# A graph layer and slice attention on one core: 35 gathers a pair of windows, halved vector operations, filler matmuls in the tail, and a wait ahead of every nine gathers

## The reference, cut to what matters

```python
# block 1
n = layernorm(x)
agg = segment_sum(n[src], dst, 6250)              # 106250 edges
h = relu(agg @ W_rel + b_rel + n @ W_root)        # 256 -> 512
i, f, g, o = split(h @ W_ih.T + b_ih + b_hh, 4)   # 512 -> 2048; f is not used
c = sigmoid(i) * tanh(g)
x = x + (sigmoid(o) * tanh(c)) @ W_fc + b_fc
# block 2, 8 heads of 64, 64 slices each
n = layernorm(x)
w = softmax((n @ W_x + b_x) @ W_slice / temp)     # slice weights per node and head
token = (w.T @ (n @ W_fx + b_fx)) / (w.sum(nodes) + 1e-5)
out_slice = attention(token W_q, token W_k, token W_v)   # 64 x 64 per head
x = x + (w @ out_slice) @ W_out + b_out
```

## Time and profile before

| | |
|---|---|
| median of 3 runs | 1493.12 us (1491.98 to 1493.93) |
| the profiled execution | 1490.67 us, its span 1488.7 us |
| TensorE matmuls busy | 1225.3 us, 82% |
| GpSimd busy | 975.0 us, 65% |
| VectorE busy | 820.7 us, 55% |
| ScalarE busy | 584.7 us, 39% |
| mean granted clock of TensorE | 0.94 of full speed |
| first and last gather start | 87.07 and 1291.05 us |

### The profile page before, as it was taken

The page is one execution under the profiler, slowest core; times in us unless marked ns, Lnnn a source line. Parts: engine busy times, 40 slices in busy tenths (PEclk is TensorE's granted clock), DMA queues, the critical chain, the costliest instruction groups (busy, mean ns, idle before and its releaser), DMA issues.

```text
span 1488.7 us, 25194 instructions
## 1 busy us (share of the span) xinstructions
PE 1225.3 (82%) x8343; PEld 1075.8 (72%) x8343; DVE 820.7 (55%) x2125; ACT 584.7 (39%) x1120; POOL 975.0 (65%) x975
## 2 busy tenths in 40 slices
PE   0226898889988898889888998989888988894796
PEld 0214787878877787778777887878777877783596
DVE  3852364656455655566555655565556645554464
ACT  3631344434443444344443444344434434352131
POOL 1247777777777777777777777777777777500043
PEclk9997999999999999999999999999999999996698
DMA  5764444444444344444444444434444444203396
GB/s 150 230 202 131 113 122 130 124 125 119 134 118 132 111 135 125 127 122 121 135 118 126 118 134 120 133 110 134 125 125 120 124 134 131 88 29 98 96 344 206
DMA packets 109102, 198.03 MB, mean 133 GB/s; under 512 B 39587, under 2 KB 66079, under 8 KB 109052
## 3 DMA queue, kind: packets, MB, share of 16 engines
q0 software_dynamic: 46160, 124.60, 29.1%
q1 hardware_dynamic: 59312, 60.26, 13.8%
q10 hardware_dynamic: 3600, 12.80, 2.1%
HBM read 165.56 MB, written 32.87 MB: 133 GB/s over the span
## 4 chain that ended last, share of the span: by engine, by line
POOL 41%; issue 30%; DMA 13%; PE 10%; DVE 3%; SPq 1%; ACT 1%; POOLq 0%; DVEq 0%; ACTq 0%
POOL ring L545 41%; DMA ring<-table,sidx 10%; PE ps L296 3%; PE ps L298 2%; PE ps L297 2%; DMA table<-ring 1%; DMA ring<-dstp 0%; SPq L337 0%; ACT ring L613 0%; PE ps L933 0%; DVE stats L1074 0%; DMA ring<-in_b_fx 0%; DMA ring<-in_x 0%; PE ps L921 0%; DMA dstp<-didx 0%
## 5 line engine op out<-in xcount | busy, mean ns | idle before, releaser
L545 POOL DMA_INDIRECT ring<-table,sidx x900 | 928.1, 1031 | 292.6 <-issue 276.9
L296 PE MATMUL ps<-h_h,wih_h 128*128 128x256 f32 x1200 | 346.7, 289 | 0.5 <-DVE h_l L1265 0.5
L297 PE MATMUL ps<-h_l,wih_h 128*128 128x256 f32 x1200 | 339.7, 283 | 0.0
L298 PE MATMUL ps<-h_h,wih_l 128*128 128x256 f32 x1200 | 339.5, 283 | 0.0
L849 PE MATMUL ps<-ring,oneh 128*125 128x512 f16 x900 | 235.2, 399 | 108.3 <-DMA ring<-table,sidx 108.2
L849 PEld LDWEIGHTS ps<-ring,oneh 128*125 128x125 f16 x900 | 120.7, 141 | 183.5 <-DMA ring<-table,sidx 132.9
L296 PEld LDWEIGHTS ps<-h_h,wih_h 128*128 128x128 f32 x1200 | 230.1, 192 | 4.2 <-issue 1.1
L297 PEld LDWEIGHTS ps<-h_l,wih_h 128*128 128x128 f32 x1200 | 230.3, 192 | 1.8
L298 PEld LDWEIGHTS ps<-h_h,wih_l 128*128 128x128 f32 x1200 | 230.2, 192 | 0.0
L679 ACT ACTIVATE gate<-ps,bgate 128x256 f32<-128x256 f32 x300 | 125.1, 468 | 189.4 <-PE ps L298 189.4
L1182 DVE TENSOR_SCALAR oneh<-iota,rel 128x125 f16<-128x125 f16 x900 | 153.3, 285 | 4.8 <-issue 3.0
(11 more groups left out here) (208 smaller groups left out, 2626.3 us busy)
## 6 DMA issues: line engine op xcount, KB each, us to landing
ring<-table,sidx POOLq DMA_INDIRECT x900, 2.8
swt_d<-swt ACTq DMA_DIRECT2D x25, 500.0 KB
gate<-swt_d SPq DMA_DIRECT2D x19, 500.0 KB, 7.1
ring<-in_x SPq DMA_DIRECT2D x12, 512.0 KB, 5.4
table<-ring SPq DMA_DIRECT2D x12, 512.0 KB, 5.4
xn<-table SPq DMA_DIRECT2D x25, 224.0 KB
xin<-in_x SPq DMA_DIRECT2D x25, 224.0 KB
res<-xin SPq DMA_DIRECT2D x25, 224.0 KB
```

The lines of the kernel that those rows point to most:

```text
L296: eng.matmul(dst, wh, xh, start=first, stop=False)
L297: eng.matmul(dst, wh, xl, start=False, stop=False)
L298: return eng.matmul(dst, wl, xh, start=False, stop=last)
L545: pool.indirect_dma_start(ring[:, e, j, :], None, table, bass.IndirectOffsetOnAxis(ap=sidx[:, e, j:j + 1], axis=0)).then_inc(done, 16)
```

## The change

- A pair has 35 slots instead of 36. The first window keeps 18 slots, and its last three (`MIX`) now hold edges from position 1920 of the pair on, whichever window they belong to. The second window has 17 slots of its own and also reads those three, so that its sum has 20 matmuls, and VectorE makes 20 matrices for it instead of 18. A pair has so 35 gathers (nine, nine, nine, eight), 38 matmuls and 38 matrices. `plan_d` checks that the lists fit, with seven more small operations. The lists of a pair come in seven DMAs (four and three) instead of four, and the second window's lists now wait for that window's sums instead of its gathers.
- Ahead of each of the four groups of a pair GpSimd now also waits for the third just before it (`PAUSES`), so that everything in front has landed; the waits on `older` stay. The first group of the first pair has no such wait. The third third of (e, k) = (0, 1) also waits for `half_used[1]`.
- The three operations over 1024 elements in the softmax, and ScalarE's exponential, become two of 512 each.
- `norm_x2` works in `xin`: b_fc is added there at the end of the turn before (`add_bfc`), and the addition of `bout` to the residual is gone; in the attention one more matmul adds `bout` to the result of head 0. ScalarE writes the normalised rows from `xin` to `x2`.
- `spin` issues matmuls whose result nobody reads: 30, 11 and 56 in turn 26 (in turn 25 none), 10 in its `token_sums`, and 25, 8, 4, 4, 28, 6, 8 and 16 between the steps of the attention.

The diff, cut to its core (left out: renamed indices, the general path, `plan_d`, the other calls of `spin`):

```diff
+    PAUSES = ((0, 0), (0, 1), (1, 0), (1, 1))
+    LISTS = (64, 48)
     CAP = CH * P
+    MIX = 3
+    OWN0 = CH - MIX
+    OWN1 = 17
+    SLOTS = OWN0 + MIX + OWN1
+    HOT1 = MIX + OWN1
+    LOW0 = OWN0 * P
+    PCAP = SLOTS * P
...
+        ring = sb("ring", [P, SLOTS, 2 * C], F16)
+        oneh = sb("oneh", [P, CH + HOT1, P], F16)
...
+        def in_group(e, k, q):
+
+            return [k * HALF + j for j in LANDS[q] if e == 0 or k * HALF + j < OWN1]
+
+        def landed(e, k, q):
+            return 16 * len(in_group(e, k, q))
...
+                if e == 0:
+                    for t, to in ((srcp, sidx[:, 0, :]), (dstp, didx[:, 0:CH])):
+                        load_list(to[:, 0:OWN0], t, base, OWN0, done)
+                        load_list(to[:, OWN0:CH], t, base + LOW0, MIX, done)
+                else:
+                    load_list(sidx[:, 1, 0:OWN1], srcp, base + CAP, OWN1, done)
+                    load_list(didx[:, CH:CH + MIX], dstp, base + LOW0, MIX, done)
+                    load_list(didx[:, CH + MIX:CH + HOT1], dstp, base + CAP, OWN1, done)
...
             def edges(p, e):
-                w = 2 * p + e
+                base = sp.value_load(base_i[0:1, ds(2 * p, 1)], min_val=0, max_val=E)
                 if not (isinstance(p, int) and p == 0):
-                    for k in range(2):
-                        for q in range(3):
-                            sp.wait_ge(rows_in[e][k][q], LAND * p)
+                    if e == 0:
+                        for k in range(2):
+                            for q in range(3):
+                                sp.wait_ge(rows_in[e][k][q], LAND * p)
+                    else:
+                        sp.wait_ge(sum_done[1], p)
                     sp.wait_ge(rel_done[e], p)
-                base = sp.value_load(base_i[0:1, ds(w, 1)], min_val=0, max_val=E)
+                    sp.sem_inc(edges_go, 1)
...
                         sp.wait_ge(res_st, 32 * p)
+                        sp.wait_ge(x2_hi, p)
...
+                            if e == 0 and k == 1 and q == 2:
+                                after(pool, half_used[1], p)
                             older = 6 * e + 3 * k + q - 2
                             if older >= 0:
                                 pool.wait_ge(rows_in[older // 6][older // 3 % 2][older % 3], LAND * p + LAND)
                             else:
-                                after(pool, rows_in[1][1][q + 1], LAND * p)
+                                after(pool, rows_in[1][1][q + 1], landed(1, 1, q + 1) * p)
+                            if q == 0 and (e, k) in PAUSES:
+                                if e or k:
+                                    pool.wait_ge(rows_in[(2 * e + k - 1) // 2][(k + 1) % 2][2], LAND * p + LAND)
+                                else:
+                                    after(pool, rows_in[1][1][2], landed(1, 1, 2) * p)
                             pool.sem_inc(gather_go, 1)
-                            for j in LANDS[q]:
-                                gather(e, k * HALF + j, rows_in[e][k][q])
+                            for j in in_group(e, k, q):
+                                gather(e, j, rows_in[e][k][q])
...
                 act.wait_ge(rstd_done, 2 * p + 2)
-                act.wait_ge(res_done, p + 1)
+                after(act, x2t_mm, p)
+                after(act, x2_hi, p)
+                after(act, x2_lo, p)
                 for e in range(2):
-                    act.activation(x2[0:WN, e, :], x2[0:WN, e, :], ACT.Identity,
+                    act.activation(x2[0:WN, e, :], xin[0:WN, e, :], ACT.Identity,
...
-                    act.wait_ge(lg_sub, t - 1)
-                    act.activation(sw[0:WN, :, :], sw[0:WN, :, :], ACT.Exp).then_inc(lg_exp, 1)
+                    for e in range(2):
+                        act.wait_ge(lg_sub, 2 * (t - 2) + e + 1)
+                        act.activation(sw[0:WN, e, :], sw[0:WN, e, :], ACT.Exp).then_inc(lg_exp, 1)
...
+                if e and k == 0:
+                    for m in range(MIX):
+                        pe.matmul(ps[0:WN, SUM_B, :], oneh[:, CH + m, 0:WN], ring[:, OWN0 + m, :],
+                                  start=(m == 0), stop=False)
                 for q in range(3):
-                    pe.wait_ge(rows_in[e][k][q], LAND * p + LAND)
-                    for i in LANDS[q]:
-                        j = k * HALF + i
-                        last = pe.matmul(ps[0:WN, SUM_A + e, :], oneh[:, e, j, 0:WN], ring[:, e, j, :],
-                                         start=(j == 0), stop=(j == CH - 1))
+                    pe.wait_ge(rows_in[e][k][q], landed(e, k, q) * p + landed(e, k, q))
+                    for j in in_group(e, k, q):
+                        hot = CH + MIX + j if e else j
+                        last = pe.matmul(ps[0:WN, SUM_A + e, :], oneh[:, hot, 0:WN], ring[:, e * CH + j, :],
+                                         start=(hot == 0), stop=(hot in (CH - 1, CH + HOT1 - 1)))
...
+                if isinstance(p, int) and p == NP - 1:
+                    spin(SUM_A, 10)
...
+            def spin(bank, n):
+
+                for _ in range(n):
+                    pe.matmul(ps[:, bank, 0:2 * P], w1_h[:, 0, 0:P], at_h[:, 0, :], start=True, stop=True,
+                              skip_group_check=True)
...
+                        spin(SUM_A, 30)
                     transpose_x2(t - 2)
...
+                        spin(SUM_A, 11)
                     logits(t - 2)
...
-                        pe.wait_ge(x2_step, 4 * (t - 2) + 1)
+                        pe.wait_ge(x2_step, 3 * (t - 2) + 2)
...
+                        spin(SUM_A, 56)
                     token_sums(t - 2)
...
+            spin(HB, 25)
             pe.wait_ge(ld_att, 16 * 6)
...
+            spin(TOK + 1, 28)
             pe.wait_ge(att_v, V_ATT)
...
+                dst = ps[u:u + G, 3 + j // 2, (j % 2) * C:(j % 2) * C + C]
+                last = pe.matmul(dst, ost[:, h * G:(h + 1) * G], wout[:, h, :], start=True, stop=(h > 0),
+                                 skip_group_check=True)
+                if h == 0:
+
+                    pe.matmul(dst, ident[0:G, 0:G], bout[0:G, :], start=False, stop=True, skip_group_check=True)
             last.then_inc(att_pe, 1)
+            spin(TOK + 1, 16)
...
-            def one_hots(e, idx, base, rel_sem, rel_n, hot_sem):
-
-                dve.tensor_scalar(rel[:, e, :], didx[:, idx, :], base, None, ALU.subtract).then_inc(rel_sem, 1)
+            def one_hots(first, n, idx, base, rel_sem, rel_n, hot_sem):
+
+                dve.tensor_scalar(rel[:, first:first + n], didx[:, idx:idx + n], base, None, ALU.subtract).then_inc(rel_sem, 1)
                 dve.wait_ge(rel_sem, rel_n)
-                for j in range(CH):
-                    last = dve.tensor_scalar(oneh[:, e, j, 0:WN], iota[:, 0:WN], rel[:, e, j:j + 1], None, ALU.is_equal)
+                for j in range(first, first + n):
+                    last = dve.tensor_scalar(oneh[:, j, 0:WN], iota[:, 0:WN], rel[:, j:j + 1], None, ALU.is_equal)
...
+            def add_bfc(p):
+                dve.wait_ge(x_in, 32 * p + 32)
+                dve.tensor_tensor(xin[0:WN, :, :], xin[0:WN, :, :], bfc[0:WN, :].unsqueeze(1).to_broadcast([WN, 2, C]),
+                                  ALU.add).then_inc(x2_step, 1)
+
             def norm_x2(p):
                 dve.wait_ge(y_mm, p + 1)
-                dve.wait_ge(x_in, 32 * p + 32)
-                after(dve, x2t_mm, p)
-                after(dve, x2_hi, p)
+                dve.wait_ge(x2_step, 3 * p + 1)
                 y = ps[0:WN, SUM_B, :].rearrange("p (e c) -> p e c", e=2)
-                dve.tensor_tensor(x2[0:WN, :, :], y, xin[0:WN, :, :], ALU.add).then_inc(x2_step, 1)
-                dve.wait_ge(x2_step, 4 * p + 1)
-                dve.tensor_tensor(x2[0:WN, :, :], x2[0:WN, :, :], bfc[0:WN, :].unsqueeze(1).to_broadcast([WN, 2, C]),
-                                  ALU.add).then_inc(x2_step, 1)
-                dve.wait_ge(x2_step, 4 * p + 2)
-                for e in range(2):
-                    dve.bn_stats(stats[0:WN, 0, e, :], x2[0:WN, e, :]).then_inc(x2_step, 1)
-                dve.wait_ge(x2_step, 4 * p + 4)
-                dve.tensor_tensor(xin[0:WN, :, :], x2[0:WN, :, :], bout[0:WN, :].unsqueeze(1).to_broadcast([WN, 2, C]),
-                                  ALU.add).then_inc(res_done, 1)
+                dve.tensor_tensor(xin[0:WN, :, :], y, xin[0:WN, :, :], ALU.add).then_inc(x2_step, 1)
+                dve.wait_ge(x2_step, 3 * p + 2)
+                dve.bn_stats(stats[0:WN, 0, 0, :], xin[0:WN, 0, :]).then_inc(x2_step, 1)
+                dve.bn_stats(stats[0:WN, 0, 1, :], xin[0:WN, 1, :]).then_inc(res_done, 1)
+                dve.wait_ge(x2_step, 3 * p + 3)
+                dve.wait_ge(res_done, p + 1)
+                dve.sem_inc(stats_go, 1)
...
-                dve.tensor_tensor(heads(sw), heads(sw), mx8[0:WN, :].unsqueeze(2).to_broadcast([WN, 2 * H, G]),
```

(56 more changed lines are left out.)

35 lines of the change are left out of this document (19 added, 16 removed).

## The result

The changed kernel takes 1651.91 us (median of 4 runs, 1650.56 to 1655.89), the kernel before 1493.53 in the same comparison: a ratio of 1.1063 [1.1039, 1.1088], 158 us slower. Forecast were 1642 us and a range of 1594 to 1686. The profiled execution took 1650.56 us.

The account below looks back on a forecast made before the run. GpSimd's stream of gathers was taken as the pace. 1490.7 - 31 (one gather less) + 225 (waits) - 33 (halves) + 1 (start) - 13 (tail) = 1639.7, with 2.4 to the median 1642 us; range 1594 to 1686 us.

Parts of the forecast that it names:

- The waits: Ahead of each group of gathers, 99 added waits lengthen a step from 1.25 to 3.52 us: +225 us, bounds 180 and 274.
- Rival A: At the added waits GpSimd restarts 0.30 us after the landing, as between ordinary gathers: 1597 us; chance 0.10.
- One gather less: Each of 25 pairs has one gather fewer on GpSimd's path, at 1.25 us each: -31 us.
- Halves: Halved softmax operations (-19), no `bout` addition (-5) and emptier pairs (-9) shorten long gathers: together -33 us, bounds 0 and -77.
- The square rule: A gather's expected wait goes with the square of the VectorE operation's length, so halving turns 50 us into 31: -19 us.
- Start: Ahead of the first gather, four lists instead of two mean two more issues of some 0.45 us: +1 us.
- Tail: Behind the gathers, fillers raise TensorE's clock, and `norm_x2` and the exponential get shorter: together -13 us, bounds 0 and -19.
- B: Gathers' landings get slower as seven lists and other stores share the queues, +0.5 us each: 1691 us; chance 0.07.
- C: TensorE becomes the bound by its clock, lowered by waits in the sums: some 1890 us; chance 0.03.
- D: Gathers themselves get short with the queues drained, 1.00 instead of 1.25 us a step: 1423 us; chance 0.02.
- E: The added waits are already met when GpSimd comes to them, so they cost nothing: 1417 us; chance 0.02.
- What to see: Signs: four 2.6 us gaps a pair, some 255 us; pairs 54 to 56 us; mean gather near 0.99; first-window waits; higher attention clock.

Follow-up runs that it names:

- first series: Four kernels made from the changed one by taking out waits, fillers, halves, or waits and halves, run beside the kernel before at 1837.0 us.
- no_spin_again: The changed kernel with spin issuing no filler matmuls, also run as no_spin: 1668.0 us, ratio 1.1154; as no_spin 1668.9 us, ratio 0.9088.
- after_again: The changed kernel itself, unaltered, run again beside the kernel before at 1495.7 us: 1659.9 us, ratio 1.1094.
- before_paused: The kernel before with only the four waits a pair added, 36 gathers, whole operations, no fillers: 1694.2 us against 1496.17.
- no_pause: The changed kernel without its added waits (PAUSES empty): 1849.7 us, ratio 1.0061; run again as no_pause_again 1412.6 us, ratio 0.9448.
- the third: The series that ran the change itself and three kernels of the first series again, beside the kernel before at 1495.7 us.
- whole: The changed kernel with the three softmax operations and the exponential whole again: 1669.9 us, ratio 0.9092; run again 1669.8 us, ratio 1.1162.

## Why the prediction was right, point by point

- **What bounds the kernel.** GpSimd is the pace before and after; what the change did to the time of the pairs shows as its idle or busy time. Upheld by every run outside the first series.
- **The waits.** Priced at 2.77 us to TensorE's start and, from two rows of the first pair, 0.75 more to GpSimd's, a step of 3.52 us. Measured over the waits: 2.80, 0.84, and 3.62 together. Forecast +225; by the trace 99 x (2.67 - 0.30) = 235, by the runs 239 of idle time and 247 in all. The missing 0.1 us a wait is mostly the restart, taken from a single pair of rows, where the mean of 72 is 0.82; 99 times 0.1 us is the 10 us by which the trace's term was missed. Rival A, a restart of 0.30 us, falls: after none of the 99 waits was GpSimd back in less than 2.53 us of idle time, and A asked for 2.1. What was worked out from the Trainium skill, DMA: Bandwidth & Descriptors, section "Anatomy of one DMA — SWDGE (gpsimd) path" (1596 us by its fixed 2.0 us and an estimated 2.3 us in all), does not agree with this trace either: the landing is 2.80 us away.
- **One gather less.** 25 x 1.25 = 31 us: 24 of busy time and 7.5 of gaps of 0.30 us. It has no run of its own, so this term is counted and not shown by an experiment; the kernel without waits comes out near a sum with it: 1493 - 31 - 9 (tail) - 38 (long gathers, 77 to 39) = 1415, measured 1412.6.
- **Halves.** Forecast -33: the long gathers fell from 77 to 40 us, -37. The size was right and the division wrong. The step that failed is the one that let halves (-24) and the emptier pair (-9) add, and that the whole came out is luck in part: waits alone take 30 us, halves alone 35, both together no more. The square rule gave 19 us for the halves where they bring 34 of busy time without waits (900.2 to 865.9). It left out that a gather needs only 0.82 us after the operation's end, 0.13 less than an undisturbed one, so that a short operation costs less than its square says. An estimate with it: a gather every 1.25 us and two operations of 0.69 us give (0.69 - 0.13)² / 1.25 = 0.25 us, times 69 is 17 us, where 17 were measured. For whole operations the same estimate gives 33 us where 50 were lost, so these don't meet the gathers at random moments.
- **Start.** Forecast +1, first gather at 87.61 instead of 87.07 us.
- **Tail.** Forecast -13, measured -8.8. The attention gave 5.5 of 7: its first 32 matmuls still take 3.30 us (3.68 before), behind a wait of 3.03 us for weights, and VectorE's work in it stayed at 12.0 us. The final loop, whose head was counted at 1.5, took 86.9 instead of 86.7 us, and of 4.9 us in front of the attention 3.5 came. The traces split it further, in us behind the last gather's end:

  | | to the attention | attention | final loop | tail |
  |---|---|---|---|---|
  | before | 81.1 | 28.9 | 86.7 | 196.7 |
  | no_spin_again | 83.6 | 29.1 | 89.7 | 202.3 |
  | after_again | 79.0 | 24.3 | 89.5 | 192.7 |
  | the change | 77.6 | 23.4 | 86.9 | 187.9 |

  So the fillers, 11.5 us of the 13 forecast, bring 9.6 to 14.4 us of tail. What went wrong is the rest, forecast at -1.9 us for `norm_x2` and the exponential: without fillers the changed kernel's tail is 5.6 us longer than the one before. `before_paused` has a tail of 199.4 us, so some 3 of these may come with the waits; the cause of the rest is open.
- **Sum.** 1642 against 1651.9: by the trace after, waits +10, tail +4, long gathers -4.
- **The other rivals.** B: landings were not slower (2.80). C: the granted clock is 0.934 over the span, TensorE waits in three of four sums, and none of GpSimd's idle time ahead of gathers is put down to it. D: a gather behind a wait takes 0.94 us (median) like the others. E: no stop of the 99 was already met.
- **What to see.** Four stops a pair: yes, 2.67 for 2.6 us, 264 for 255; pairs of 54 to 56: yes, a steady one 54.9 for 55.0; mean gather 0.991 for 0.99; waits in the first window's sums: yes; clock in the attention 0.93.

## What to carry to other kernels

Where an engine that issues DMAs is the pace, a wait until everything issued has landed costs the whole way to landing plus the restart, less one ordinary step: here 3.62 - 1.25 = 2.4 us a time by the trace, 2.5 by the runs, for something that nothing behind it needed. Wait for the oldest landing that is needed, not for the newest: one gather later the same wait costs 1.0 to 1.1 us, and without the waits the change takes 0.9448 of the kernel before. In the first series the waits had another worth (next section), so a comparison of this kind is worth repeating. Two remedies for the same loss aren't added: ask what the second finds left of it.

## What the runs showed of the hardware that was not expected

- **The same kernel at 1413 and at 1850 us.** `no_pause` and `no_pause_again` are one kernel; its ten runs of the first series all lie between 1835 and 1863 us, the four of the third between 1409 and 1416. The kernel before moved with it, 1837 and 1496. Kernels with a stop every nine gathers did not move: 1668.9 and 1668.0, 1669.9 and 1669.8. What grew is idle time in the middle of TensorE's matmuls with nothing waited for, 299 us against 3, and their own time, by 146 us at a granted clock of 0.863 against 0.980. That TensorE there lacked instructions, and that the stream of gathers was in the way of their coming, is argued and wasn't shown. What set this series apart is open; the record gives it the same chip number as the third, so by this number it isn't one chip against another. While it lasts, the verdict turns: at a ratio of about 0.91 for the near relatives of the change, `no_spin` and `whole`, the waits save time.
- **A waiting GpSimd starts later than a waiting TensorE**, by 0.84 us on the same landing (median of 72; 0.75 to 0.87 by the place in the program), though between gathers it needs only 0.30 us. Why it differs by place is open.
- **Stops in the stream shorten the gathers**, from a mean of 1031 to 998 ns in `before_paused`: 21 of VectorE's 69 long operations begin during a stop, and the time that gathers lose inside the 69 falls from 50 to 28 us.
